# New order tables for all five engines of a fused feed-forward, mixer, feed-forward kernel

## What is computed

```python
# FFN: every batch picks 2 of 8 experts from the mean of its tokens
seq_rep = hidden_states.mean(axis=1)
probs = softmax(seq_rep @ gate_w); top_w, top_i = top_k(probs, 2)
hmid = gelu(einsum('bth,hf->btf', hidden_states, w1[e]) + b1[e])      # 128 -> 512
y = einsum('btf,fh->bth', hmid, w2[e]) + b2[e]                        # 512 -> 128
out = out + combine[:, e][:, None, None] * y
# mixer
xc = silu(conv4(rmsnorm(x)));  dt_raw, v, gate_raw = split(xc @ in_proj_w, 3)
dt = clip(softplus(dt_raw + dt_bias), 0.001, 2.0);  v_in = rope(v) * dt
L = clip(cumsum(-dt) within 32 tokens, -20, 0)                        # running sum 1
cum_decay = clip(cumsum(L at chunk ends), -80, 0)                     # running sum 2
final = decayed sum of v_in within chunks + carries between chunks    # two scans
out = x + (head_mix(final) * sigmoid(gate_raw)) @ out_proj_w
```

## Time and profile before

| | us |
|---|---|
| median of 3 runs | 260.31 (260.23 to 260.34) |
| the profiled execution, its time | 260.13 |
| its span on the core | 258.3 |
| TensorE busy | 251.7 (97%) |
| VectorE busy | 211.1 (82%) |
| ScalarE busy | 195.1 (76%) |
| GpSimd busy | 82.9 (32%) |
| granted TensorE clock, mean | 0.997 of full |

### The profile page before, as it was taken

The page is one execution under the profiler, slowest core; times in us unless marked ns, Lnnn a source line. Parts: engine busy times, 40 slices in busy tenths (PEclk is TensorE's granted clock), DMA queues, the critical chain, the costliest instruction groups (busy, mean ns, idle before and its releaser), DMA issues.

```text
span 258.3 us, 4609 instructions
## 1 busy us (share of the span) xinstructions
PE 251.7 (97%) x1540; PEld 218.6 (85%) x1540; DVE 211.1 (82%) x536; ACT 195.1 (76%) x236; POOL 82.9 (32%) x90
## 2 busy tenths in 40 slices
...
DMA packets 21975, 26.18 MB, mean 101 GB/s; under 512 B 1280, under 2 KB 17152, under 8 KB 21952
## 3 DMA queue, kind: packets, MB, share of 16 engines
...
## 4 chain that ended last, share of the span: by engine, by line
PE 91%; ACT 3%; issue 2%; DMA 1%; DVE 1%; POOL 0%; SPq 0%; DVEq 0%; ACTq 0%; POOLq 0%
PE hid_ps L845 32%; PE y_ps L873 28%; PE y_ps L898 10%; PE aux_ps L984 5%; PE aux_ps L940 4%; PE aux_ps L1016 3%; PE aux_ps L1005 3%; PE hid_ps L1023 2%; PE y_ps L917 1%; PE aux_ps L965 1%; ACT hid L639 1%; DMA m_tok<-wpack_dram 1%; ACT late L729 1%; PE y_ps L1028 1%; PE hid_ps L917 1%
## 5 line engine op out<-in xcount | busy, mean ns | idle before, releaser
L845 PE MATMUL hid_ps<-z_hi,w_parts 128*128 128x512 f32 x256 | 83.9, 410 | 0.4 <-ACT w_parts L592 0.4
L873 PEld LDWEIGHTS y_ps<-w_sb,hid 128*128 128x128 f32 x640 | 77.1, 192 | 4.3 <-DMA w_sb<-wpack_dram 0.8
L873 PE MATMUL y_ps<-w_sb,hid 128*128 128x128 f32 x640 | 78.1, 275 | 0.4 <-ACT hid L639 0.4
L639 ACT ACTIVATE hid<-hid_ps,w_sb 128x1024 f32<-128x1024 f32 x56 | 61.8, 1109 | 16.7 <-PE hid_ps L845 16.4
L845 PEld LDWEIGHTS hid_ps<-z_hi,w_parts 128*128 128x128 f32 x256 | 45.2, 189 | 9.5 <-issue 1.4
L845 PE MATMUL hid_ps<-z_lo,w_parts 128*128 128x512 f32 x128 | 40.1, 394 | 0.0
L1223 DVE TENSOR_TENSOR hid_lo<-hid,hid_hi 128x1024 fp32r<-128x1024 f32 x19 | 22.9, 1218 | 7.8 <-ACT hid_hi L646 7.8
L845 PEld LDWEIGHTS hid_ps<-z_lo,w_parts 128*128 128x128 f32 x128 | 24.0, 188 | 5.6
L646 ACT ACTIVATE hid_hi<-hid 128x1024 fp32r<-128x1024 f32 x19 | 19.6, 1054 | 1.3 <-PE y_ps L898 1.2
L486 POOL TENSOR_SCALAR bias_tok<-w_sb,coef 128x128 f32<-128x128 f32 x10 | 7.3, 734 | 39.1 <-DMA w_sb<-wpack_dram 25.2
L1110 DVE TENSOR_SCALAR f_tok<-xt,f_mv,f_rstd 128x128 f32<-128x128 f32 x64 | 17.7, 351 | 2.0 <-POOL f_rstd L464 1.9
...
## 6 DMA issues: line engine op xcount, KB each, us to landing
...
```

Source lines behind the costliest of these rows:

```text
L639: nc.scalar.activation(hid[:, slot % HBUF, :], hid_ps[:, slot % 2, :], ACT.Gelu, bias=bias).then_inc(hid_ready, 1)
L845: last = nc.tensor.matmul(hid_ps[:, slot % 2, cols], w, z[:, q % 2, cols], start=first, stop=end)
L873: last = nc.tensor.matmul(y_ps[:, cols], hid[:, slot % HBUF, cols], w_sb[:, q % 2, k, W2_AT + f * P:W2_AT + (f + 1) * P], start=t == 0 and ...
```

## The change

All numbers of the table `AT` are set anew, for all passes, batches and engines. No job is added, removed or altered, and the fixed ticks of the slots stay. All changed lines of the diff are of this kind; these hold the places that are spoken of below:

```diff
     "pe": {
...
-        "m_dt": {0: 649, 1: 1029, 2: 1349, 3: 1726},
+        "m_dt": {0: 709, 1: 1029, 2: 1389, 3: 1766},
...
     "dve": {
...
-        "m_dstep": {0: 737, 1: 1189, 2: 1484, 3: 1914},
-        "m_carry": {0: 778, 1: 1183, 2: 1527, 3: 1912},
+        "m_carry": {0: 777, 1: 1134, 2: 1515, 3: 1940},
+        "m_dstep": {0: 779, 1: 1172, 2: 1528, 3: 1887},
...
     "act": {
-        "c_split_rest": {0: 19, 1: 60},
+        "c_split_rest": {0: 60, 1: 100},
...
-        "m_dt": {0: 660, 1: 1020, 2: 1346, 3: 1730},
+        "m_dt": {0: 700, 1: 1026, 2: 1380, 3: 1744},
...
-        "m_decay": {0: 780, 1: 1180, 2: 1540, 3: 1933},
+        "m_decay": {0: 780, 1: 1173, 2: 1533, 3: 1910},
```

More of the change, by code:

```diff
@@ L59 @@
-        "y_turn_y": {5: 2206, 6: 2426, 7: 2600},
+        "f_norm": {1: 169, 2: 349, 3: 809, 4: 1149, 5: 1509, 6: 1829, 7: 2166},
+        "f_route": {1: 189, 2: 389, 3: 929, 4: 1189, 5: 1549, 6: 1860, 7: 2186},
+        "m_norm": {0: 529, 1: 889, 2: 1209, 3: 1489},
+        "m_dt": {0: 709, 1: 1029, 2: 1389, 3: 1766},
+        "m_v": {0: 749, 1: 1069, 2: 1409, 3: 1786},
+        "m_gate": {0: 869, 1: 1249, 2: 1569, 3: 1906},
+        "m_heads": {0: 909, 1: 1289, 2: 1669, 3: 2046},
+        "m_out": {0: 949, 1: 1349, 2: 1726, 3: 2066},
@@ L81 @@
-        "m_silu_lo": {0: 640, 1: 1018, 2: 1345, 3: 1698},
-        "m_decay": {0: 694, 1: 1075, 2: 1413, 3: 1779},
-        "m_dstep": {0: 737, 1: 1189, 2: 1484, 3: 1914},
-        "m_carry": {0: 778, 1: 1183, 2: 1527, 3: 1912},
[L85 to L89, removed]
@@ new lines @@
+        "f_split_w1": {1: 285},
+        "f_coef": {1: 416, 2: 700, 3: 1037, 4: 1293, 5: 1661, 6: 1990, 7: 2281},
+        "f_bias": {5: 1942, 6: 2150, 7: 2535},
+        "m_stats": {0: 423, 1: 721, 2: 1042, 3: 1362},
+        "m_normalise": {0: 505, 1: 844, 2: 1148, 3: 1411},
+        "m_clip": {0: 558, 1: 905, 2: 1252, 3: 1509},
[3 rows of a table added]
+        "m_silu": {0: 651, 1: 979, 2: 1332, 3: 1675},
+        "m_silu_lo": {0: 689, 1: 1015, 2: 1352, 3: 1757},
+        "m_decay": {0: 742, 1: 1082, 2: 1430, 3: 1798},
@@ new lines @@
+        "m_carry": {0: 777, 1: 1134, 2: 1515, 3: 1940},
+        "m_dstep": {0: 779, 1: 1172, 2: 1528, 3: 1887},
+        "m_cos": {0: 794, 1: 1136, 2: 1468, 3: 1817},
+        "m_sin": {0: 807, 1: 1122, 2: 1500, 3: 1837},
+        "m_u": {0: 819, 1: 1191, 2: 1516, 3: 1910},
+        "m_u2": {0: 833, 1: 1208, 2: 1543, 3: 1948},
+        "m_scan": {0: 864, 1: 1232, 2: 1592, 3: 1972},
+        "m_scan2": {0: 883, 1: 1258, 2: 1633, 3: 1994},
+        "m_gated": {0: 918, 1: 1322, 2: 1700, 3: 2062},
```

89 lines of the change are left out of this document (37 added, 52 removed), and 6 rows, old and new, of the table AT.

## The result

The changed kernel takes 264.78 us (median of 6 runs, 264.35 to 265.25), the kernel before 260.22 in runs beside it: 1.018 times as long, 95% interval 1.0161 to 1.0198. Predicted were 264.9, from 260.6 to 266.8. The profiled execution takes 264.91 with a span of 263.0, against 260.13 and 258.3 before. The total came out as forecast; its parts did not all.

The account below looks back on a forecast made before the run. TensorE, busy for 251.7 of 258.3 us, was taken as the bound, so only its waits count. Terms of -0.47, +0.8, +0.6 and +3.7 sum to +4.63 on 260.13; with 0.18 for the median, 264.9 us, range 260.6 to 266.8.

Parts of the forecast that it names:

- Start: At the first jobs, gelu 0 ahead of the split starts earlier and `down` 0 follows: -0.47 us.
- Batch 0, 74 to 90 us: GpSimd's three operations fall under VectorE's work, taking 4.55 instead of 1.16 and delaying ScalarE and `m_rms`: +0.8 us.
- Batch 3, `m_dt`: `m_dt` later on TensorE delays ScalarE's Exp and gelu 43, so `down` 43 starts later: +0.6 us.
- Batch 3, `m_decay` and `m_carry`: Late `cumd` and slowed GpSimd make ScalarE wait for `small`, with gelu 47 and `down` 47 behind: +3.7 us.
- One step each: Rival: GpSimd's operations each wait for only one VectorE step; +1.6 in place of +3.7, 262.8 us; chance 0.2.
- GpSimd is not held up: Rival: each chain of three GpSimd operations takes 1.2 us in batches 0 and 3; 260.2 us; chance 0.12.
- Faster: Rival: GpSimd unhindered and gelu 43 done when `down` 43 is reached, -0.86 there; 258.8 us; chance 0.1.

Follow-up runs that it names:

- A: The changed kernel itself, with the whole new order; 264.78 us. Its family is the kernels made from it by further edits.
- B: The kernel before the change; 260.22 us beside the changed kernel. Its family is the kernels made from it by single edits.
- a_sin: The changed kernel with VectorE's `m_sin` of batch 0 ahead of `m_cos` (793 in place of 807); 265.63 us, with B at 259.28 beside it.
- a_warm: The changed kernel with the six matmuls of `up` 48 issued three times, filling TensorE's idle time; 263.05 us, with B at 259.28 beside it.
- b_place3: B with only batch 3's `m_decay` ahead of gelu 47 on ScalarE and `cumd` later on VectorE; 265.18 us, with B at 259.63 beside it.
- a_cumd: The changed kernel with VectorE's `cumd` of batch 3 back ahead of `dstep` (1886 in place of 1940); 259.83 us, with B at 259.63 beside it.
- a_mid2: The changed kernel with VectorE's `cumd` of batch 3 right behind `dstep` (1888 in place of 1940); 259.82 us, with B at 259.30 beside it.

## Why the prediction was right, and where it was not

Term by term, from the starts of the same jobs in the two traces:

| term | predicted | measured |
|---|---|---|
| up to `up` 0 | 0 | -0.47 |
| *Start* | -0.47 | -0.33 |
| *Batch 0, 74 to 90 us* | +0.8 | -0.24 |
| 130 to 140 us | 0 | +0.25 |
| *Batch 3, `m_dt`* | +0.6 | +0.65 |
| *Batch 3, `m_decay` and `m_carry`* | +3.7 | +5.1 |
| the tail | 0 | -0.3 |
| sum | +4.63 | +4.66 |

- **Start.** Right in mechanism, mis-sized by 0.14: gelu 0 started 1.82 us after `up` 0 (13.79 - 11.97), and I had taken 1.70 (14.14 - 12.44). `down` 0 came at 15.05, earlier than the 15.4 named, since `up` 0 itself started at 11.97. That 0.47 is no effect of the order: `up` 0 lies between 11.39 and 12.11 in the nine profiles of A's family and between 11.46 and 12.44 in the five of B's. From `up` 0 on the new order costs 5.17 us, more than the medians say.
- **Batch 0.** The step that failed is "So GpSimd's three operations now lie under VectorE's work: 4.55 in place of 1.16". They took 1.97. I had argued that VectorE is never idle there and not looked at what its steps read: L531 and L534 fell under `m_cos`, which takes one input from PSUM. a_sin shows that this made the difference for L531. The trace of before has the sign of it. VectorE is not idle all through the earlier trace rows:

```profile
76.94 1.22 DVE L1362 TENSOR_TENSOR late<-aux_ps,rope_sb 128x1024 f32<-128x1024 f32 x1 [0.83 <-ACT late L729]
```

  This is `m_cos`, and L534 at 77.11 ran its 0.24 beneath it. ScalarE's wait was mis-sized too: it came to the Exp of `small` at 79.28, so that 4.55 us from 74.99 on (79.54) would have held it up by 0.3 at most. ScalarE's table load and Exp covered what the operations took, and the VectorE wait for `m_inv` at 81 us that I had named did not come. What went is the 0.2 at `down` 19.
- **`m_dt`.** The traces have +0.51 at `down` 43 itself and 0.14 around it, against +0.6. The Exp started at 180.00 in a trace that ran 0.8 early there, so at 180.8 counted as the prediction counts (180.76).
- **`m_decay` and `m_carry`.** The chain is the one predicted, link for link: `cumd` late, L531 over two VectorE steps, L534 under the scan, `small` at 201.42, 3.25 us of waiting on ScalarE, a table load and the gelu. `small` was taken at 201.95, some 0.4 too late with the 0.1 that the trace runs early there: `cumd` was done at 196.55, not at 197.0 to 197.2, and the three operations took 4.79. (By the prediction's own terms the upper end is 197.2 + 4.55 + 1.1 = 202.85 and not 202.4.) TensorE lost 3.33 us in the wait, 3.7 were taken. What the term lacked, and its upper bound of 4.2 with it, is the clock: another 1.75 us, shown by a_warm. No row of before gives a price for it. But that trace does show the clock at half 2.1 us behind TensorE's last matmul (254.8 and 256.9), and I had forecast a wait of 3.7 us where TensorE had none over 0.6 between its slots: that should have widened the bound.
- **The sum** is right to 0.03 us by luck: a cost that was not seen (+1.75) is nearly cancelled by a term that did not come (+0.8), by the wait that was 0.4 shorter than taken and by the early `up` 0. Its sign and its place are well founded: b_place3 gives it alone, a_cumd and a_mid2 take it away.
- **The rivals.** "One step each" fails on L531, 2.30 us here and 2.2 to 2.55 in every run at this place. "GpSimd is not held up" holds for batch 0 and not for batch 3. "Faster" fails, as reckoned, at the Exp of batch 3 (180.00, needed before 179.3).

The +0.25 at 130 to 140 us is open: no wait stands there in either trace, the same jobs follow each other in another order. The tail's -0.3 lies behind TensorE's last matmul, where the last stores run: 3.2 us in each of the nine profiles of A's family (in A from 259.79 to 263.01), 3.6 in each of the five of B's (254.77 to 258.33). So it belongs to the new order, in a term that the prediction had at 0; which line gives it is open.
